# Layer 0 experts: rows gathered by computed token numbers instead of rows scattered to slots

## The reference, cut to what matters

```python
capacity = int(math.ceil(T / E * 1.25))            # T = 4096 tokens, E = 8 experts: 640
probs = jax.nn.softmax(tokens @ router_w.T, axis=-1)
top1_idx, top1_prob = jnp.argmax(probs, -1), jnp.max(probs, -1)
order = jnp.lexsort((-top1_prob, top1_idx))        # per expert, most probable first
...
keep = pos_in_group < capacity                     # the others fall back to expert 0
final_e = jnp.where(keep, top1_idx, 0)
for e in range(E):
    h = jax.nn.relu(tokens @ W1[e] + b1[e])        # 128 -> 512
    y = h @ W2[e] + b2[e]                          # 512 -> 128
    out = out + jnp.where((final_e == e)[:, None], y, 0.0)
```

## Time and profile before

| what | value |
|---|---|
| median of 3 runs | 1595.36 us |
| the profiled execution, its own time | 1594.38 us |
| span of its trace | 1592.6 us |
| PE busy | 1364.1 us, 86% |
| DVE busy | 1065.8 us, 67% |
| ACT busy | 820.6 us, 52% |
| POOL busy | 678.8 us, 43% |
| mean granted TensorE clock | 0.947 of full speed |

### The profile page before, as it was taken

How to read it: one execution, slowest core, us unless ns; L and a number is a source line. 1 busy time by engine, 2 the same in 40 slices (tenths; PEclk the granted TensorE clock), 3 DMA queues, 4 the chain that set the end, 5 groups by cost and what they waited for, 6 DMA issues and landing times. The chain is left out here.

```text
span 1592.6 us, 44968 instructions
## 1 busy us (share of the span) xinstructions
PE 1364.1 (86%) x14646; PEld 1017.9 (64%) x14646; DVE 1065.8 (67%) x3426; ACT 820.6 (52%) x2400; POOL 678.8 (43%) x1293
## 2 busy tenths in 40 slices
PE   4888888868669599999999999987999999985981
PEld 2666666646457466666666666656777777764970
DVE  3899899846103258777777777765777777773433
ACT  2565566533223267777777777763443444331640
POOL 2455555420624324444444444442223444444773
PEclk9999999969879889999999999998999999996995
DMA  6566733200111211222222121200000000002425
GB/s 201 176 192 205 229 112 116 85 1 1 50 48 50 89 66 60 73 62 75 68 65 73 60 73 60 73 28 3 1 1 11 14 13 10 14 21 65 114 81 166
DMA packets 86300, 115.57 MB, mean 73 GB/s; under 512 B 12418, under 2 KB 64650, under 8 KB 86096
## 3 DMA queue, kind: packets, MB, share of 16 engines
q1 hardware_dynamic: 79536, 102.55, 20.2%
q0 software_dynamic: 6688, 12.07, 2.3%
HBM read 78.97 MB, written 37.32 MB: 73 GB/s over the span
## 5 line engine op out<-in xcount | busy, mean ns | idle before, releaser
L1741 ACT ACTIVATE c_pr<-c_pS,c_nm 128x257 f32<-128x257 f32 x512 | 238.2, 471 | 95.0 <-DVE c_nm L1877 95.0
L1877 DVE TENSOR_REDUCE c_nm<-c_pS 128x1 f32<-128x257 f32 (+1 forms) x384 | 173.3, 506 | 40.2 <-PE c_pS L1621 39.4
L2199 ACT ACTIVATE s_k<-s_pK 128x512 f32<-128x512 f32 x128 | 76.4, 597 | 177.9 <-PE s_pK L2096 177.9
L1625 PE MATMUL c_pT<-cst,c_pr 128*128 128x128 f32 x1024 | 163.2, 284 | 0.0
L2096 PE MATMUL s_pK<-s_hT,AH 128*128 128x128 f32 x1024 | 137.4, 284 | 0.5 <-ACT s_hT L2194 0.5
L2096 PEld LDWEIGHTS s_pK<-s_hT,AH 128*128 128x128 f32 x1024 | 123.9, 195 | 21.4 <-ACT s_k L2199 18.2
L1625 PEld LDWEIGHTS c_pT<-cst,c_pr 128*128 128x128 f32 x1024 | 111.5, 142 | 37.7 <-issue 37.7
L2117 PE MATMUL s_pM<-BH,s_uT 128*128 128x128 f32 x1024 | 121.7, 278 | 1.3 <-DVE LG L2351 1.3
L2117 PEld LDWEIGHTS s_pM<-BH,s_uT 128*128 128x128 f32 x1024 | 118.7, 195 | 1.7 <-DVE LG L2351 1.7
L1886 DVE COPY c_prT<-c_pT 128x512 f32<-128x512 f32 x128 | 88.6, 692 | 26.8 <-PE c_pT L1625 21.4
L1621 PE MATMUL c_pS<-c_ks,c_qq 32*128 32x257 f32 x1024 | 95.3, 431 | 12.9 <-POOL c_qq L1793 8.7
(11 more groups left out here) (358 smaller groups left out, 3276.2 us busy)
## 6 DMA issues: line engine op xcount, KB each, us to landing
rows_in<-c_blank SPq DMA_DIRECT2D x32, 520.0 KB, 2.9
a_ctxT<-in_ctxT SPq DMA_DIRECT2D x32, 514.0 KB, 3.7
c_ctxT<-in_ctxT SPq DMA_DIRECT2D x128, 128.5 KB, 2.1
a_ctxN<-in_ctxR SPq DMA_DIRECT2D x32, 512.0 KB, 4.2
f_hb<-rows_in SPq DMA_DIRECT2D x39, 130.0 KB
f_w<-in_f_w SPq DMA_DIRECT2D x16, 256.0 KB, 3.4
f_back<-rows_out SPq DMA_DIRECT2D x16, 256.0 KB, 5.6
rows_in<-a_zero SPq DMA_DIRECT2D x7, 322.5 KB, 4.5
```

What stands on the lines that cost most here:

```text
L1625: mm = pe.transpose(pT[:, c, j, :], pr[:, b % 2, j, c * P:(c + 1) * P], k("ident"))
L1741: act.activation(pr[:, b % 2, c, :], pS[:, c, 0:S], ACT.Exp, bias=nm[:, c:c + 1], accum_out=den[:, b % 2, c:c + 1]).then_inc(e_ready.sem, 1)
L1877: dve.tensor_reduce(nm[:, c:end], pS[:, c:end, 0:S], AX.X, ALU.max, negate=True).then_inc(max_ready.sem, 1)
L2199: act.activation(k2[:, c * HK:(c + 1) * HK, :], pK[:, c % 2, :, :], ACT.Copy).then_inc(k_ready.sem, 1)
```

## The change

The token numbers of each expert's slots are computed on the chip, and the rows are gathered from DRAM by them.

- `attend_layer0`: `H_all` has rows of 128; the token column, its iota and its copy go; `rows_in` goes, with its seven zero writes.
- `route_layer0`: SP writes `H_all` to a new DRAM tensor `rows_h`, one row per token, in 8 DMAs. POOL makes the tables `lanes` (0 to 127) and `token` (token number minus 8192). DVE splits each slot into `block_of` (slot / 128) and `lane_of` (slot modulo 128), three steps more.
- `experts_layer0`: DVE builds one-hot tables in four chunks of 8 groups: `in_block` [128, 8, 35] and `in_lane` [128, 8, 128] (in the space of `H_all`). POOL multiplies `in_block` by `token`. PE, behind `up(0)`, sums the products of both over 32 groups into `pN` [128, 35]. DVE adds 8192 and casts: `token_of`, with 8192 (out of bounds) for an empty slot. DVE also clears `h`, which has three buffers now. POOL then gathers 5 x 128 rows per expert by indirect DMA from `rows_h`, experts 1 to 3 at once and expert e + 3 ahead of the result scatter of expert e. The 32 scatters and the 7 loads on SP are gone.

```diff
+RINGS = 3                       # SB = SLOTS // P = 35
@@ attend_layer0
-                if e > 0:
-                    sp.dma_start(env["rows_in"][(e - 1) * CAP:e * CAP, :].rearrange("(k p) d -> p k d", p=P),
-                                 zero[:, :, :]).then_inc(env["rows_zeroed"], 16)
...
-            pool.memset(zero[:, :, D:DR], NO_TOKEN).then_inc(zeroed.sem, 1)
-            pool.iota(token[:, :], [[1, G]], base=0, channel_multiplier=G).then_inc(token_ready.sem, 1)
-            pool.wait_ge(token_ready.sem, 1)
-            pool.tensor_copy(H_all[:, :, D], token[:, :])
@@ route_layer0
+        @block.sync
+        def _(sp):
+            rows_h = env["rows_h"].rearrange("(p g) d -> p g d", g=G)
+            for n in range(NB):
+                r = slice(n * TG, (n + 1) * TG)
+                sp.dma_start(rows_h[:, r, :], env["H_all"][:, r, :]).then_inc(env["h_stored"], 16)
...
+            pool.iota(lane_i[:, :], [[1, P]], base=0, channel_multiplier=0).then_inc(numbers_ready.sem, 1)
+            pool.iota(token_i[:, :], [[1, G]], base=0, channel_multiplier=G).then_inc(numbers_ready.sem, 1)
+            pool.wait_ge(numbers_ready.sem, 2)
+            pool.tensor_copy(lanes[:, :], lane_i[:, :])
+            pool.tensor_copy(token[:, :], token_i[:, :]).then_inc(numbers_ready.sem, 1)
+            pool.wait_ge(numbers_ready.sem, 3)
+            pool.tensor_scalar(token[:, :], token[:, :], -float(2 * TOKENS), None, ALU.add)
...
-            then(dve.tensor_copy(halves(slot_of[:, :]), turned))
+            then(dve.tensor_copy(halves(slot_i[:, :]), turned))
+            then(dve.tensor_single_scalar(slot_i[:, :], slot_i[:, :], 7, ALU.logical_shift_right))
+            then(dve.tensor_copy(block_of[:, :], slot_i[:, :]))
+            then(dve.scalar_tensor_tensor(halves(lane_of[:, :]), halves(block_of[:, :]), -float(P), turned, ALU.mult, ALU.add))
@@ experts_layer0, sync
-            sp.wait_ge(scattered, 16 * G)
-            for e in range(1, E):
-                if e > 2:
-                    sp.wait_ge(hT_done, e - 2)
-                    sp.wait_ge(token_ready, e - 2)
-                sp.dma_start(h[:, e % 2, :, :], rows(rows_in, e)).then_inc(h_loaded[e % 2], 16)
@@ experts_layer0, tensor
+            def token_numbers():
+                for g in range(G):
+                    if g % GC == 0:
+                        pe.wait_ge(in_lane_ready, g // GC + 1)
+                        pe.wait_ge(in_block_ready, g // GC + 1)
+                    mm = pe.matmul(pN, in_lane[:, g, :], in_block[:, g, :], start=(g == 0), stop=(g == G - 1))
+                mm.then_inc(number_done, 1)
             def dense():
                 up(0)
+                token_numbers()
                 for r in range(LATE):
...
             def turn(e):
-                pe.wait_ge(h_loaded[e % 2], 16 * ((e + 1) // 2))
+                pe.wait_ge(h_loaded[e % RINGS], 16 * NT * ((e - 1) // RINGS + 1))
@@ experts_layer0, gpsimd
-            pool.wait_ge(env["rows_zeroed"], 16 * (E - 1 + G))
-            for g in range(G):
-                pool.indirect_dma_start(rows_in, bass.IndirectOffsetOnAxis(ap=slot_of[:, g:g + 1], axis=0), H_all[:, g, :], None,
-                                        bounds_check=SLOTS - 1, oob_is_err=False).then_inc(scattered, 16)
+            def gather(e):
+                for i in range(NT):
+                    j = (e - 1) * NT + i
+                    pool.indirect_dma_start(h[:, e % RINGS, i, :], None, rows_h, bass.IndirectOffsetOnAxis(ap=token_of[:, j:j + 1], axis=0),
+                                            bounds_check=G * P - 1, oob_is_err=False).then_inc(h_loaded[e % RINGS], 16)
...
+            for c in range(CHUNKS):
+                numbers_of_groups(c)
+            pool.wait_ge(env["rows_zeroed"], 16 * G)
+            pool.wait_ge(env["h_stored"], 16 * NB)
+            pool.wait_ge(h_cleared, 1)
+            pool.wait_ge(token_ready, 1)
+            for e in range(1, RINGS + 1):
+                gather(e)
+            for e in range(1, E):
+                if e + RINGS < E:
+                    pool.wait_ge(hT_done, e)
+                    gather(e + RINGS)
+                scatter(e)
@@ experts_layer0, vector
+            dve.wait_ge(env["h_stored"], 16 * NB)
+            for c in range(CHUNKS):
+                blocks_of_groups(c)
+                lanes_of_groups(c)
+            dve.memset(h[:, :, :, :], 0.0).then_inc(h_cleared, 1)
+            token_numbers()
             dve.wait_ge(b2_loaded, 16)
...
-                    dve.wait_ge(h_loaded[e % 2], 16 * ((e + 1) // 2))
-                    dve.tensor_copy(token_of[:, e, :], h[:, e % 2, :, D]).then_inc(token_ready, 1)
```

More of the change, by code:

```diff
@@ L174, in build_program @@
         env["y0"] = sb("y0", [P, DENSE * TG, D], c=routed)
+        env["lane_of"], env["block_of"] = sb("lane_of", [P, G], c=routed), sb("block_of", [P, G], c=routed)
+        env["lanes"], env["token"] = sb("lanes", [P, P], c=routed), sb("token", [P, G], c=routed)
         route_layer0(env)
@@ L267, in attend_layer0 @@
         pOs = pO[:, 0:NQ * W].rearrange("p (c e) -> p c e", c=NQ)
-        zero = sb("zero", [P, NT, DR])
-        token = sb("token", [P, G], I32)
+        zero = sb("zero", [P, D])
         n1 = Norm(ctx, nc, "a_n1", env)
@@ L645, in _ @@
             ins.then_inc(ones_ready.sem, 1)
[L646 to L650 removed]
+            pool.memset(zero[:, :], 0.0).then_inc(zeroed.sem, 1)
             def add_bias(x):
@@ L831, in route_layer0 @@
 def route_layer0(env):
-    nc, LG, MASK, slot_of, k, vec = (env[n] for n in ("nc", "LG", "MASK", "slot_of", "k", "vec"))
+    nc, LG, MASK, k, vec = (env[n] for n in ("nc", "LG", "MASK", "k", "vec"))
+    lane_of, block_of, lanes, token = (env[n] for n in ("lane_of", "block_of", "lanes", "token"))
     gamma1, HT_all, y0, (w1, w2) = env["gamma1"], env["HT_all"], env["y0"], env["ew"][0]
@@ L1062, in experts_layer0 @@
         hid = sb("hid", [P, 2, NF, CAP])
-        h, hT, y = sb("h", [P, 2, NT, DR]), sb("hT", [P, 2, CAP]), sb("y", [P, 2, NT, D])
-        back = HT_all
-        token_of = sb("token_of", [P, E, NT], U32)
+        h, hT, y = sb("h", [P, RINGS, NT, D]), sb("hT", [P, 2, CAP]), sb("y", [P, 2, NT, D])
+        back, in_lane = HT_all, env["H_all"]
+        in_block, number, token_of = sb("in_block", [P, G, SB]), sb("number", [P, SB]), sb("token_of", [P, SB], U32)
+        CHUNKS = 4
+        GC = G // CHUNKS
         PIECES, AT_ONCE = 14, G // (E - 1) + 1
@@ L1071, in experts_layer0 @@
         pY = ps("pY", [P, 2, 4, D])
-        b2_loaded, scattered, gathered = (ctx.semaphore("f0_b2_loaded"), ctx.semaphore("f0_scattered"),
-                                          [ctx.semaphore(f"f0_gathered{n}") for n in range(NB)])
-        h_loaded = [ctx.semaphore(f"f0_h_loaded{p}") for p in range(2)]
+        b2_loaded, gathered = ctx.semaphore("f0_b2_loaded"), [ctx.semaphore(f"f0_gathered{n}") for n in range(NB)]
+        h_loaded = [ctx.semaphore(f"f0_h_loaded{p}") for p in range(RINGS)]
+        found, in_block_ready, in_lane_ready = ctx.semaphore("f0_found"), ctx.semaphore("f0_in_block_ready"), ctx.semaphore("f0_in_lane_ready")
+        number_done, number_ready, h_cleared = ctx.semaphore("f0_number_done"), ctx.semaphore("f0_number_ready"), ctx.semaphore("f0_h_cleared")
         y_scattered = [ctx.semaphore(f"f0_y_scattered{p}") for p in range(2)]
@@ L1255, in _, with numbers_of_groups @@
         def _(pool):
-            pool.wait_ge(env["rows_zeroed"], 16 * (E - 1 + G))
-            for g in range(G):
-                pool.indirect_dma_start(rows_in, bass.IndirectOffsetOnAxis(ap=slot_of[:, g:g + 1], axis=0), H_all[:, g, :], None,
-                                        bounds_check=SLOTS - 1, oob_is_err=False).then_inc(scattered, 16)
-            for e in range(1, E):
+            def numbers_of_groups(c):
+                r = slice(c * GC, (c + 1) * GC)
+                pool.wait_ge(found, c + 1)
+                pool.tensor_tensor(in_block[:, r, :], in_block[:, r, :], token[:, r].unsqueeze(2).broadcast_to([P, GC, SB]), ALU.mult
+                                   ).then_inc(in_block_ready, 1)
```

53 lines of the change are left out of this document (35 added, 18 removed).

## The result

The changed kernel takes **1583.13 us** (median of 5 runs, 1582.4 to 1585.55) against 1595.36 us (5 runs, 1592.74 to 1597.72): ratio 0.9914, 95% interval 0.9897 to 0.9931, so 12.2 us less. The forecast was 1578.2 us, in a range of 1573 to 1587. The time is inside that range and 5 us above the forecast; it lies outside the forecast's own range of 1575 to 1581.5, where the prediction had put rival (a), whose middle was 1584.6.

What follows compares the result with a forecast made beforehand. The prediction took PE's 22 us hole in layer 0's experts, waiting for h, as the bound. 14.0 us from an earlier turn(1) plus 3.2 us of clock make 17.2: 1595.36 - 17.2 = 1578.2 us, range 1573 to 1587.

Steps and rivals of the forecast that it cites:

- rival (a): PE's clock falls over the token products; gain 4 to 9.6 us smaller, middle 1584.6 us; chance 0.15.
- (b): Gathers on POOL are dearer, 1.5 to 2.1 us each; time 1580 to 1588 us; chance 0.12.
- What bounds the kernel: Layer 0's experts: PE's hole of 22 us, waiting for a load of h behind POOL's scatters, lies on the one path.
- Attention's zero writes at 0: Attention block: leaving out seven zero writes, covered by DVE and PE, gains 0 to 1 us, taken as 0.
- Routing block: SP's stores and POOL's tables are covered and count 0; three small DVE steps behind the cast are not.
- DVE's three steps at 0.65 us: End of routing, behind the cast: three small uncovered steps cost 0.6 to 0.75 us, taken as 0.65.
- The tables: Experts' block: DVE needs 1.67 us per chunk, POOL keeps up; chunk 4 ready near 411 us, so PE does not wait.
- Token products at 7.4 us: Ahead of up(1) on PE: 64 records cost 6 to 8.5 us, taken as 0.115 each, 7.4 us.
- Hole gone, 14.0 us, and clock 3.2 us: turn(1) starts at 435.4 instead of 449.38 us, 14.0 us earlier; PE arrives at 2.4 GHz, saving 3.2 us more.
- POOL keeps up, with 1.2 us to spare: Alternating scatters and gathers, the last gathers land at 496.4 us, before turn(7) wants them at 497.6.
- (c): POOL's queue becomes the bound above 2.21 us per gather; at 2.6 us the time is 1609 us; chance 0.05.

Runs made afterwards that it cites:

- number 2: Changed kernel with the seven zero writes, their memset and the wait for them put back: 1581.67 us.
- number 4: Changed kernel with the 32 token products in four parts of 8, each before one of the four products of up(1): 1581.45 us.
- number 3: Kernel before the change, with 94 unread products of 128 columns keeping PE busy in its hole: 1592.55 us, ratio 0.9987.
- Numbers 6 and 7: 6: changed kernel with every gather issued twice, 1617.33 us in a single run; 7: changed kernel with two buffers of h instead of three, 1603.08 us.
- numbers 8 and 12: Changed kernel with token products in four parts; 8 adds 50 unread products at the block's end, 1580.73 us; 12 adds one idle DVE write, 1579.24 us.

## Why the prediction was right in kind and 5 us off in size

- **The number.** That it lies in the range is due to the room given to rivals (a) and (b): rival (a) came true at half its price, and 2.0 us that no term had came on top. The forecast alone, with its own range, missed.
- **What bounds the kernel**: held. The hole was on the path, and taking it out moved everything behind it.
- **Attention's zero writes at 0**: held by the medians (number 2), which cannot tell 1 us from none.
- **Routing block**: DVE's three steps at 0.65 us: MASK to PE's first product is 402.11 - 399.90 = 2.21 us, was 1.53: 0.68. SP's stores and POOL's tables are hidden.
- **The tables**: PE waited for none, as forecast, but not for the reason given, that 280 elements take POOL less than 1.07 us: its product took 1.56 us, and DVE's compare 0.90 instead of 0.45 when the two met. The last table product was still done at 408.50 + 1.57 = 410.1 us, some 3 us before PE came to the last chunk. The Trainium skill (SBUF — State Buffer, section on who interferes with whom) says that a DVE instruction with two SBUF inputs contends with GpSimd's reads, and the trace agrees, with these numbers. I had weighed this rule for the gathers alone, where it takes little: 1.05 to 1.13 us instead of 1.00 in a few of them.
- **Token products at 7.4 us: the step that failed.** At full clock they are 6.8 us (number 4), a little less than I took. What I left out of the sum, and had as rival (a) at 0.15 with 4 to 9.6 us, is the fall of the clock: in the two profiles it made them 8.16 and 8.62 and `up(1)` 5.77 and 5.28 us, where number 4 has 6.8 and 4 x 0.94 = 3.8: together 3.3. The mechanism is the rival's and the size lies below its lower end, as the clock fell only 6 us into the products and rose again 7 us later, while the rival's upper end has half clock over all of them. "PE's queue has no gaps" was true and did not help. The Trainium skill (TensorE: Matmul & The Clock Gate, Part 1) ties the clock to how busy PE has been; here PE shows as busy throughout, with records of 35 columns, and yet the clock fell. The trace does not agree with the page as far as these rows measure how busy PE is; number 3's 128-column records, as gapless and at the same pace, kept the clock.
- **Hole gone, 14.0 us, and clock 3.2 us**: 3.1 by the stage, 3.0 by number 3 (2.7 and 2.6 against the second profile of the kernel before). Of the 14.0 the token products took back 2.7: 3.3 for the clock, less the 0.6 by which they were cheaper than taken. `turn(1)` comes 436.21 - 402.11 = 34.1 us after the block's first product, not 31.4.
- **POOL keeps up, with 1.2 us to spare**: held. The last gather starts at 494.46 and is issued by 495.5 (forecast: 493.9), and `turn(7)` at 498.56 (forecast: 497.6) waits for nothing. Numbers 6 and 7 show how thin the cover is. Rivals (b) and (c) did not happen; a gather is 1.30 us in a row, against 1.28 taken.
- **Sum.** Predicted 17.2; less 2.7 for the token products and some 0.3 in small terms is 14.2, which the stage from MASK to the read back shows; the measured difference is 12.2, so 2.0 went elsewhere, and no term had them. From the read back to the end the two profiles of the code before have 1050.9 and 1053.8 us, those of the changed kernel 1055.1 and 1055.5, which is 1.3 to 4.6 more; ahead of MASK the changed kernel's have 0.6 to 2.0 us less. Self attention alone is 3.5 to 4.6 us longer in them. That the 2.0 us of the medians are these is likely, not shown, and why the clock there is lower stays open.

## What to carry to other kernels

A row of small products with few columns (here 64 records of 35) between big ones can drop TensorE's clock although PE never idles; put them piecewise between larger products and look at the granted clock, not at the busy share. When indirect DMAs replace another load, count the whole queue of the issuing engine per round (here 10 x 1.30 = 13 us on POOL against PE's 11.13 us per expert: only the lead from the third buffer covers it) and where each one stands relative to the waits in front of it. Where a wait appears, count the half clock behind it too: here it added 3.5 us to each wait of 5. And take gains read off one stage at a few microseconds less than full: a stage behind that nobody touched moved by up to 5.5 us from profile to profile.

## What the runs showed of the hardware that was not expected

- The clock fell from 2.4 to 1.2 GHz at 414 us with PE busy for 1.00 of 1.00 us for 6 us before it; with two larger records between each 16 small ones it did not, and 188 gapless records of 128 columns at nearly the same pace (0.113 us each, against 0.107) left it at 2.4 GHz.
- A POOL product and a DVE compare, both from SBUF, took 1.56 and 0.90 us together; alone the compare took 0.45.
- An indirect gather of 128 rows costs POOL the same as a scatter: 1.00 us busy and 1.30 from one to the next, against 0.98 and 1.29.
- The self attention of layer 1 took 383.1 to 388.6 us with the same instructions, in step with the granted clock around its start. The Trainium skill (TensorE: Matmul & The Clock Gate, Part 1) says that the clock's decision runs freely and does not start anew with the kernel. The profiles fit that (numbers 8 and 12 start the stage at the same time and differ by 2.2 us), but do not prove it.
